# V's last three passes and its read one unit later in the steps without an output product, and the second mask ahead of k's rope in three of them

## The reference

```python
xn = _layernorm(x)
# attention, per batch of 512 tokens
q, k, v = proj(Wq), proj(Wk), proj(Wv)            # xn @ W.T, 16 heads of 32
q, k = _apply_rope(q, k)                          # q * cos + rotate_half(q) * sin
scores = where(causal, q @ k.T / sqrt(32), min)
attn = softmax(scores) @ v @ Wo.T
# experts, per token
top_vals, top_idx = top_k(xn @ gate_w.T, 2)
ffn = sum over the two of softmax(top_vals) * (xn @ expert_w[e].T + expert_b[e])
out = x + attn + ffn
```

## Time and profile before

| | us |
|---|---|
| median of 3 runs | 995.77 |
| the profiled execution, whole | 1002.43 |
| its span | 1000.6 |
| PE busy in it | 932.2 (93%) |
| DVE busy | 746.0 (75%) |
| POOL busy | 555.9 (56%) |
| ACT busy | 435.6 (44%) |
| mean granted clock of PE | 0.98 |

### The profile page before, as it was taken

One profiled execution on the slowest core, in us unless ns is written; L12 is line 12 of the kernel. 1 busy time (PEld: TensorE's weight loads), 2 busy tenths in 40 slices (PEclk: granted clock), 3 DMA queues, 4 the chain that ended last, 5 costly groups with the idle time before them and its releaser, 6 DMA issues.

```text
span 1000.6 us, 18754 instructions
## 1 busy us (share of the span) xinstructions
PE 932.2 (93%) x6589; PEld 448.1 (45%) x6589; DVE 746.0 (75%) x1327; ACT 435.6 (44%) x711; POOL 555.9 (56%) x553
## 2 busy tenths in 40 slices
PE   2899888988999999989999999989999999999897
PEld 1344334444444444535555555534444444444333
DVE  7888987887889899944444444477788888788865
ACT  5267865855755443331112211224434444344432
POOL 1545575574575556662333333247877888777641
PEclk9999999998999999999999999999999999999989
DMA  6366588698587344395655555454555554555431
GB/s 239 106 222 214 158 277 303 181 305 300 175 264 291 123 159 138 142 313 167 201 175 175 178 169 176 158 205 149 187 175 180 178 191 139 162 186 179 142 107 54
DMA packets 107963, 188.63 MB, mean 189 GB/s; under 512 B 11872, under 2 KB 65248, under 8 KB 102624
## 3 DMA queue, kind: packets, MB, share of 16 engines
q1 hardware_dynamic: 97072, 152.03, 44.1%
q0 software_dynamic: 10800, 35.40, 12.4%
HBM read 117.13 MB, written 70.25 MB: 187 GB/s over the span
## 4 chain that ended last, share of the span: by engine, by line
PE 68%; DVE 12%; DMA 7%; POOL 6%; ACT 4%; issue 2%; SPq 1%; DVEq 0%; ACTq 0%; POOLq 0%
PE psum L947 18%; PE psum L1032 11%; PE psum L1056 6%; PE psum L995 6%; PE psum L982 6%; PE psum L1041 5%; PE psum L998 5%; PE psum L964 5%; DMA x_in<-x 4%; PE psum L924 3%; DVE top L1482 3%; PE psum L966 2%; POOL gT L579 1%; POOL k_hl L588 1%; DMA xT_rows<-gT 1%
## 5 line engine op out<-in xcount | busy, mean ns | idle before, releaser
L760 ACT ACTIVATE pT<-psum,factors 128x512 f32<-128x512 f32 (+1 forms) x352 | 219.6, 640 | 253.8 <-PE psum L982 234.0
L1482 DVE TENSOR_REDUCE top<-psum 128x1 f32<-128x384 f32 (+3 forms) x352 | 210.5, 634 | 23.4 <-PE psum L966 22.4
L1032 PE MATMUL psum<-xT,w_att 128*128 128x512 f16 x768 | 197.5, 383 | 6.9 <-DVE xT L1433 5.0
L947 PE MATMUL psum<-w_exp,x_gT 128*128 x852 | 197.0, 381 | 0.9 <-issue 0.9
L964 PE MATMUL psum<-k_stack,q_stack 96*128 96x384 f16 (+3 forms) x512 | 128.8, 305 | 19.6 <-DVE top L1482 18.8
L608 POOL DMA_INDIRECT x_g<-xn_rows,tok_of x71 | 67.5, 951 | 135.8 <-PE psum L924 134.3
L982 PE MATMUL psum<-q_stack,k_stack 98*128 98x256 f16 (+3 forms) x512 | 129.3, 305 | 6.0 <-ACT pT L760 4.7
L1438 DVE TENSOR_TENSOR x_gT<-psum,x_gT 128x512 f16<-128x512 f32 x71 | 49.1, 692 | 105.2 <-ACT x_gT L784 85.1
L947 PEld LDWEIGHTS psum<-w_exp,x_gT 128*128 128x128 f16 x852 | 83.7, 98 | 87.2 <-issue 3.4
L784 ACT ACTIVATE x_gT<-psum 128x512 f16<-128x512 f32 x71 | 42.5, 598 | 172.2 <-PE psum L924 170.2
L592 POOL TENSOR_SCALAR_AFFINE_SELECT pT<-pT 128x512 f32<-128x512 f32 x128 | 94.8, 751 | 20.4 <-ACT pT L760 20.4
(11 more groups left out here) (175 smaller groups left out, 1282.9 us busy)
## 6 DMA issues: line engine op xcount, KB each, us to landing
y_rows<-y_sb SPq DMA_DIRECT2D x71, 256.0 KB
w_in<-w_all SPq DMA_DIRECT2D x12, 1024.0 KB, 9.6
q_stack<-qk_rows SPq DMA_DIRECT2D x96, 128.0 KB
k_stack<-qk_rows SPq DMA_DIRECT2D x96, 128.0 KB
x_in<-x SPq DMA_DIRECT2D x8, 1024.0 KB, 13.3
qk_rows<-q_hl SPq DMA_DIRECT2D x32, 256.0 KB
qk_rows<-k_hl SPq DMA_DIRECT2D x32, 256.0 KB
xn_rows<-x_in SPq DMA_DIRECT2D x8, 1024.0 KB, 4.9
```

Of the source, the lines that this page charges most:

```text
L760: act.activation(p_of(j, h, heads), banks[BANK_T + (NT_ * n + k) % 2][:, 0:W], ACT.Exp, scale=factors[:, 0:1]).then_inc(exp_done, 1)
L947: now = pe.matmul(banks[s % 4], x_gT[s % 4][:, xp * C + c, :], w_exp[:, bass.ds(e, 1), wp, c, :].rearrange("p e d -> p (e d)"), start=n == ...
L1032: now = pe.matmul(bank, w_att[:, what, wp, c, g * P:(g + 1) * P], xT[b % 2][:, xp * C + c, :], start=at_pass == 0, stop=at_pass == 3 * C - 1)
L1482: return dve.tensor_reduce(out=top[:, h:h + heads, i], in_=banks[BANK_S + k % 2][:, 0:heads * W].rearrange("p (h t) -> p h t", h=heads), a ...
```

## The change

In the steps whose `out_tiles(n)` is empty, passes 9 to 11 of V's product move from ahead of c's turn to behind shifted unit 8, and on ACT V's read moves from ahead of exp 8 to behind it. In steps 0, 1 and 15 the mask of block 1 moves ahead of k's rope on POOL, as it is in steps 13 and 14 already. No instruction is added or dropped, and no size changes.

```diff
--- before.py
+++ after.py
@@ -272,6 +272,7 @@
     TAKE_AT = {4: 2, 6: 3, 10: 4}
     JOB_AT = {n: i for i, n in enumerate((0, 1, 2, 4, 5, 7, 8, 9, 10), 3)}
     CHOOSE = N1 - 5
+    MASK_FIRST = (0, 1, CHOOSE + 2, CHOOSE + 3, N1 - 1)
 
 
 
@@ -636,11 +637,11 @@
                 if n + 3 < N:
                     low_qk(0, n + 3)
 
-                if n in (CHOOSE + 2, CHOOSE + 3):
+                if n in MASK_FIRST:
                     mask(n, 1)
                 if n + 3 < N:
                     rope(1, n + 3)
-                if n not in (CHOOSE + 2, CHOOSE + 3):
+                if n not in MASK_FIRST:
                     mask(n, 1)
                 if n >= N1 and n + 1 < N:
                     gather_y(late_tiles(n + 1)[1])
@@ -812,9 +813,13 @@
                 exps(n, 7)
                 if n + 1 < N:
                     copy_c(n + 1)
-                if n + G < N:
+                if out_tiles(n):
+                    if n + G < N:
+                        take_v(n + G, BANK_QV)
+                    exps(n, 8)
+                else:
+                    exps(n, 8)
                     take_v(n + G, BANK_QV)
-                exps(n, 8)
                 if n + 3 < N:
                     high_qk(1, n + 3)
                 if n in TURN_AT:
@@ -1175,10 +1180,12 @@
                 if not nxt:
                     project_out(N - 2, OUT_LAST[2], 6, 9)
                 if vs:
-                    project_v(n + G, BANK_QV, 6, 12)
+                    project_v(n + G, BANK_QV, 6, 12 if wo else 9)
                 if nxt:
                     turn_c(n + 1)
                 shifted_scores(n, 8)
+                if vs and not wo:
+                    project_v(n + G, BANK_QV, 9, 12)
                 if wo:
                     pe.wait_ge(o_lo, G * b)
                     if ahead:
```

## The result

| | before | after |
|---|---|---|
| median, us | 994.83 | 998.11 |
| lowest to highest, us | 989.33 to 998.64 | 994.53 to 1004.65 |
| executions | 20 | 20 |
| the profiled execution, us | 1002.43 | 998.92 |

The ratio is 1.0040, with a 95% interval of 1.0025 to 1.0054: the change makes the kernel some 4 us slower, a little more than the 3 us that the prediction had as the least that can be told from nothing. Single executions of either kernel lie up to 10 us apart. The profiled execution of before happened to be one of the slow ones of its kernel, so the span after (997.1 us) is even shorter than the earlier trace rows. The two spans can't be set against each other; stretches of them can.

What follows compares the result with a forecast made beforehand. No one engine was taken to bound a step: PE (busy 93%), DVE and ACT in turn. Terms -0.6 + 2.3 + 1.0 + 0 - 0.4 = +2.3 us on 995.8 gave 998.1 us, range 994.6 to 1001.0.

Steps and rivals of the forecast that it cites:

- rival B: Clock bites behind both new gaps, in steps 1 (1.9 us) and 15: +4.1 us, about 1000.2 us; chance 22%.
- The sign, "slower": Whole kernel: slower by more than 3.0 us, over 998.8 us, 0.36; same 0.54; faster, under 992.8 us, 0.10.
- Step 0, -0.6: Step 0: k's high half 1.27 us later, PE idles 1.2 us, DVE early; -0.6 us, bounds -0.95 and +0.3.
- Step 1, +2.3 without the clock: Step 1: late mask makes exps 9 and 10 3.0 us later, PE idles nearly 4 us; +2.3 us, low bound +0.7.
- The clock, +1.0: Behind step 1's idle time PE runs at 1.2 GHz, costing up to 1.9 us or nothing; +1.0 us, the middle.
- Steps 2 and 3, 0: Steps 2 and 3: PE gains 0.4 us, gives it back at the next wait; 0, between -0.2 and +0.3 each.
- Step 15, -0.4: Step 15: c's turn near 429.8, then PE idles about 2 us for a gather; -0.4 us, bounds -3.6 and +0.5.
- Rival A: Step 1's idle time comes without the clock's cost, and step 15 gives 1.3 us: +0.4 us, 996.2 us; chance 30%.
- Rival C: Step 15: second gathered tile lands before 434 and step 1 costs only 0.7 us: -3.5 us, 992.3 us; chance 12%.

Runs made afterwards that it cites:

- steps 0 and 15 alone: V late and mask first in steps 0 and 15 only, against the kernel before: 994.64 us, ratio 0.9995; a second time 995.16 us, ratio 1.0011.
- the mask alone: The kernel before with only the mask of block 1 ahead of k's rope in step 1, V unmoved: 999.07 us against 996.07, ratio 1.0029.
- steps 2 and 3 alone: The kernel before with V late in steps 2 and 3 only, no mask moved: 996.34 us against 995.17, ratio 1.0004.
- Step 15 alone: The kernel before with V late and mask first in step 15 only: 994.32 us against 996.07, ratio 0.9991.

## Why the prediction was right, and where it was too small

998.1 us was forecast and 998.11 measured, but the agreement to a hundredth is luck: the kernel before came out 0.9 us lower in the runs beside it than in the three shown, and the difference measured is 3.3 us by the medians and 4.0 by the ratio, where +2.3 was forecast. It falls between the forecast and rival B. The upper end of the range, 1001.0, is 0.5 us above what its own terms give (995.8 + 4.1 + 0.6 = 1000.5), which nothing rests on. The sign, "slower", was given 0.36 against 0.54 for no difference that can be told. Step by step:

- **Step 0, -0.6.** Forecast: k's high half at 79.65, PE's wait 1.2 us. Measured 79.66 and 1.22. The step's gain by c's turn of step 1 is 0.46 us (the two runs of steps 0 and 15 alone: 46.07 and 46.06 us against 46.53). Right, a little less than forecast.
- **Step 1, +2.3 without the clock.** Forecast: ACT idle about 3 us, PE's wait near 3.9. Measured 3.27 and 3.69, and with the mask alone the time from c's turn of step 1 to the spread of the maximum grew from 7.41 to 9.81 us: +2.40. Right, and shown in both directions. Part of the reasoning was the lock between POOL and DVE: the mask ended 0.5 us after W's low part, as forecast. The Trainium skill, "SBUF — State Buffer", section "Who interferes with whom", has a DVE instruction with two inputs in SBUF contend with a GpSimd one that reads SBUF, and calls the ports that both use an exclusive lock; the mask's 2.33 us beside DVE's low part of W, against 0.63 in step 0, agree.
- **The clock, +1.0.** From the spread to the normalisation it took 3.23 us (twice) and 3.20 us, not 1.93: +1.3 us in all three profiles that have this mask. That is within the bounds, nearer their upper end, where I took the middle. What the bounds left out is that the low stretch can last 6.8 us: in the profile of the change it runs on into the projections, and from the normalisation to c's turn of step 2 are 13.37 us instead of 12.02. In the two others it lasts 3.4 us and that part has 12.10. So the mask of step 1 cost 3.8 us in two profiles and 5.1 in one (21.99 being the interval without it), where the sum had 3.3. This is the term that was too small.
- **Steps 2 and 3, 0.** c's turn in step 2 does not move: 67.94 us from the prologue's turn against 67.89, with V late in steps 2 and 3 alone. PE gives back what it gains, as forecast. But the sum had no clock here, and the wait it gives the time back in grew from 1.17 to 1.73 us, behind which the clock fell in four of seven profiles. A term of some +1.0 on average was missing, by the estimate above the other part of what the sum had too little; steps 2 and 3 alone measured +0.4 us with 1.8 either way, which can't confirm it.
- **Step 15, -0.4.** c's turn came 1.7 us earlier, as worked out (about 429.8; 429.90), and PE then waited for the second gathered tile, 1.32 us of the 2 forecast. By the first expert product some of it is given back. Counted from c's turn of step 14 that product starts after 30.9 us on average in the ten profiles with the mask first in step 15 (30.6 to 32.4) and after 31.6 us in the four without (30.8 to 32.3), 0.8 us earlier. How much is kept to the end I can't say. From c's turn of step 15 to that of step 16, across the expert tiles, took between 242.2 and 250.6 us in the 14 profiles, and on average no less in the ten (245.8) than in the four (244.9). Step 15 alone measured -0.9 us with 2.4 either way.

Put together, the terms as the profiles have them are -0.5 (step 0), +4.2 (step 1 with its clock, the mean of 3.8, 3.8 and 5.1), +1.0 (steps 2 and 3) and -0.8 (step 15): +3.9 us, where the two runs of the change measured +4.0 and +5.2 by their ratios. The direction and the path were forecast rightly; the terms of the clock were too small.

Rival A fails at the clock. Rival C fails at both of its conditions: the second gathered tile was not there before 434 (PE waited for it until 434.96), and the mask of step 1 costs 2.4 us, not its low bound of 0.7. Rival B had the right price for step 1 (1.9 us at the clock were its term; 1.3 to 2.7 measured), and its second place, step 15, is met in some executions: a low stretch lies at the gather's wait in two of the ten profiles with the mask first there. The stretch from 434 us on is at the full clock in the profile of the change; in that of step 15 alone the level is low behind the gather's wait (1.74 us); first the change, then step 15 alone:

```profile
434.00:441.00 7.00, 5.13 (x52) 2.99 (x53) 3.76 (x6) 2.77 (x5) 4.66 (x6) 1.00 0.68 172
```

```profile
431.90:435.30 3.40, 3.40 (x35) 1.64 (x28) 1.03 (x2) 0.38 (x1) 1.93 (x2) 0.50 0.67 190
```

What stays open is the small change around zero. V's part, step 0 and step 15, together or apart, came out between 0.9978 and 1.0015 of before in seven comparisons, each 0.002 to 0.003 wide to either side. Whether they give half a microsecond or two, these runs can't show.

## What to carry to other kernels

When an operation is put ahead on an in-order engine, follow what it pushes back through every queue to the end of the chain, not to its own consumer: here a mask ahead of a rope delayed a cast on ACT, behind which stood a sum that another engine's whole queue waited for. A cure that worked here is to move the held operation behind the urgent ones, on each engine of the chain, and to order SP's DMA queue by when its inputs are now ready. And where single executions scatter by several microseconds, judge a change of one or two by intervals between the same instructions in several profiles, and by one part of it at a time.

## What was unexpected on the chip

- The low clock is not a fixed toll. Behind nearly the same wait (3.69, 3.67 and 3.62 us) it lasted 6.8 us once and 3.4 us twice; behind 1.73 us it came in four profiles of seven. The Trainium skill, "TensorE: Matmul & The Clock Gate", section "HAM oscillation — how this bites in real kernels", warns of waits longer than the 1.73 us; here waits of 1.73 us bring it too, now and then, which is one source of the scatter of 10 us between executions of one kernel. In the 14 profiles PE spent between 13.6 us (steps 0 and 15 alone, the second time, the shortest span, 987.6 us) and 42.9 us (before, span 1000.6 us) at the low level. It isn't the only source: the longest span, 1001.3 us, has 34.3 us of it and the slowest stretch of expert tiles (250.6 us). The profiled execution of before had such stretches from 178.2 on (3.4 us) and from 226.0 on (6.8 us), in steps that the change leaves alone, that of after only one from 227.3 on (3.4 us). From c's turn of step 4 to that of step 5 are 25.74 us before and 23.06 after, from step 6 to 7 28.87 and 26.14: 5.4 us by which the slower kernel's profile looks the faster.
- A very small operation can pay for a long neighbour. c's product on 16 columns took 0.4 us in step 2 and 1.44 or 2.66 us in step 15, and this operation on 4 columns, beside a rope in step 0 of the change, 1.11 us (0.29 us in step 1):

```profile
78.66 1.27 POOL L585 TENSOR_TENSOR plain_k<-plain_k,turned_k 128x512 f32<-128x512 f32 x1
78.84 1.11 DVE L1303 TENSOR_SCALAR var_eps<-mean_var 128x4 f32<-128x4 f32 x1
```
